# A two-layer decoder on one core: the first layer's maxima subtracted in four row groups, a shorter expert table, and a new order of steps

## The chip, the core and the metric

The kernel runs on one core of a Trainium2 chip. The core has five engines with an instruction queue each: TensorE (PE in the profile; its weight loads are PEld), VectorE (DVE), ScalarE (ACT), GpSimd (POOL) and SyncE (SP), which here only starts transfers. The metric is the device time of one execution in microseconds. Lower is better. The kernel before took 615.67 us, the median of three runs (613.36 to 617.16).

## The reference

The input x has 8 sequences of 256 positions by 256 features. The output is x after six steps, each of the form `x = layernorm(x + step(x))`. Cut to what matters, with all heads 16 wide:

```python
# layer 0
x = ln(x + x @ (Wr + Wc) + bias)                    # mixing with decay matrices
s = (q @ k.T) / sqrt(16)                            # q from x, k and v from 64 context rows; 16 heads
x = ln(x + softmax(where(causal, s, min)) @ v @ Wout)
e = argmax(x @ router_w)                            # one of 8 experts per token
x = ln(x + expert[e](x * sigmoid(max logit)) + shared_expert(x))
# layer 1
x = ln(x + ifft(normed(fft(q)) * cumsum(normed(fft(k)))) @ W_o)
x = ln(x + attention over the 64 context rows (rotary, low rank) )
x = ln(x + rms_norm(silu(x @ Wg) * (x @ Wu)) @ Wp)  # weights rounded to three values
```

A softmax is computed as exp(score - maximum) over its sum. The maximum of each query and head has to be taken off all the head's scores. This is where the change works.

## The kernel before, in words

A sequence is a unit. Units 0 to 7 are the eight sequences in layer 0, and units 8 to 15 are the same eight in layer 1. Five units of layer 0 are in work at a time, and four of layer 1. Between the two layers, all tokens go through the experts: each token's row is sent to a slot of its expert (`rk_send`, an indirect DMA from POOL), a small table says which 128 slots form each of 23 tiles and which expert owns them (`tb_cnt`, `tb_tile`), the tiles are loaded (`x_ld`), multiplied, stored, and gathered back per token (`gt`, indirect DMAs from POOL).

The program is cut into some 2300 steps with short names and (unit, part) numbers. Each step belongs to one engine. `lay_plan` (L334) lists them with a length in units of 10 ns, the steps that they wait for, and the PSUM banks that they need (there are eight). `RANKS` (L173) is a string of two characters for each step that says how urgent it is. `Plan.lay` (L270) walks through time with these lengths and ranks and so fixes, before anything runs, the order of the steps on each engine and the bank of each. On the chip each engine works through its list and waits at each step for the semaphores of that step. A step that is late holds up everything behind it on its engine.

`keep_warm` (L240) then looks for gaps of 0.8 us or more between two PE steps of that plan, and puts filler matmuls into 0.7 of each gap: 128x512 products whose result nobody reads (`warm`, L1418). Its last argument is the time of the plan from which it does so, 9 us.

The steps that matter here, for a unit u:

- Layer 0: `kv`, `turn`, `proj` 0 with `ln` 0, `q`, `max` (scores for the maxima, on PE), `max_v` (the maxima, on DVE, L1913), `mt` (the maxima turned so that heads are rows, L1263), `mt_c` (copied to SBUF by ACT), `sc` (all scores again, minus the maxima, L1268), `ex_h`, `ex_f` and `ex_l` (the exponential and its split), `pv`, `ot`, `proj` 1, then the router `rt`, `rt_top`, `rt_hot` (a one-hot row per token, DVE), `rk` (PE: how many tokens before this one went to the same expert), `rk_seen` (DVE: the running count per expert, L1979), `rk_slot` (DVE: the token's slot), `rk_send` (POOL), and the shared expert `sh`, `sh_h`, `hs_lo`, `proj` 2, `res`, `st_mid`.
- In `sc` of layer 0 four banks are written. A score needs a contraction over 32 rows only, and the four banks' products use different 32 rows of the array (L1277). Then each bank gets the causal mask (L1280, one matmul) and two matmuls that take the maxima off (L1282). These two contract over all 128 rows: `minus_head` has -1 in one of 16 rows and zeros elsewhere.
- `tb` (L1366) sums the counts over the partitions on PE, and `tb_cnt` and `tb_tile` (L2007, L2018) make the table from it with small VectorE instructions. `dve.step` makes the engine wait for its own instruction before the next one.
- Between the layers POOL runs `gt` for four units, `rope` (eight small instructions per unit), and `ln_pow` (the power in the layernorm), which releases `ln_x` on ACT and with it `turn` and `ft` on PE.

## Time and profile before

| | |
|---|---|
| median of 3 runs | 615.67 us (613.36 to 617.16) |
| the profiled execution's own time | 610.82 us |
| its span in the profile | 609.5 us |
| granted TensorE clock, mean | 0.99 |
| PE, DVE, ACT, POOL busy | 553.6, 472.8, 369.8, 389.4 us |
| instructions | 14270 |

The span is the time from the first to the last instruction of the profiled execution. The busy share of PE counts a matmul from its start to its modelled end, so matmuls that follow each other overlap, and a busy PE isn't an engine that has no room. The fillers count as busy too. The start of one matmul less the start of the one before says more.

### The profile page before, as it was taken

How to read it: one execution, taken by the hardware profiler on the slowest of the kernel's cores; microseconds unless marked ns; L12 is line 12 of the kernel's file. 1: busy time of each engine (PE TensorE's matmuls, PEld its weight loads, DVE VectorE, ACT ScalarE, POOL GpSimd, SP SyncE). 2: the span in 40 equal slices, each digit the busy share in tenths (PEclk: the TensorE clock that was granted, in tenths of full speed). 3: DMA queues.
4: the chain of work that ended last, by engine and by line, in shares of the span. 5: the costliest groups of instructions: out<-in, count | busy, mean ns of one | idle time of the engine just before them, and what ended most of it. 6: DMA issues, size and time to landing. Idle time of an engine off the chain costs nothing. (4 is left out here: it accounts for less than half of the span.)

```text
span 609.5 us, 14270 instructions
## 1 busy us (share of the span) xinstructions
PE 553.6 (91%) x5331; PEld 436.6 (72%) x5331; DVE 472.8 (78%) x1266; ACT 369.8 (61%) x783; POOL 389.4 (64%) x467
## 2 busy tenths in 40 slices
PE   5789999889777999977899999999999999999995
PEld 3657887768654766643477888887877778889994
DVE  6896978796889675568899586689888898867656
ACT  5767588667643644545376567647665666655663
POOL 5839657678770440079999938775686644343896
PEclk9998999999899999999899999999999999999999
DMA  9132223104657443472010000022001200000001
GB/s 351 46 140 91 69 74 121 40 24 140 194 173 225 128 146 104 160 170 37 0 31 3 2 1 2 2 54 53 2 20 34 52 3 1 2 1 3 1 2 69
DMA packets 23696, 42.19 MB, mean 69 GB/s; under 512 B 3834, under 2 KB 18300, under 8 KB 23612
## 3 DMA queue, kind: packets, MB, share of 16 engines
q1 hardware_dynamic: 19900, 35.56, 17.9%
q0 software_dynamic: 3072, 4.20, 3.4%
q10 hardware_dynamic: 656, 1.52, 0.8%
q8 instruction: 43, 0.70, 0.5%
q14 instruction: 25, 0.20, 0.1%
HBM read 31.96 MB, written 10.35 MB: 69 GB/s over the span
## 5 line engine op out<-in xcount | busy, mean ns | idle before, releaser
L1761 DVE TENSOR_TENSOR first<-bank,first 128x512 f16<-128x512 f32 (+2 forms) x127 | 69.7, 564 | 14.0 <-ACT first L1627 5.9
L2216 POOL TENSOR_TENSOR first<-first 128x512 f16<-128x512 f32 x44 | 52.5, 1197 | 22.4 <-ACT first L1648 19.7
L1070 PE MATMUL bank<-wide,first 128*128 128x256 f16 (+4 forms) x199 | 54.3, 283 | 8.7 <-DVE first L1761 3.2
L1077 PE MATMUL bank<-c_first,first 128*128 128x128 f32 (+1 forms) x318 | 51.4, 280 | 3.8 <-ACT first L1580 1.8
L1071 PE MATMUL bank<-wide,first 128*128 128x256 f16 (+4 forms) x199 | 54.1, 282 | 0.0
L1072 PE MATMUL bank<-wide,first 128*128 128x256 f16 (+4 forms) x199 | 53.1, 281 | 0.0
L1077 PEld LDWEIGHTS bank<-c_first,first 128*128 128x128 f32 (+1 forms) x318 | 36.3, 140 | 12.2 <-ACT first L1580 4.7
L2194 POOL TENSOR_TENSOR first<-first,minus_half 128x2 f32<-128x2 f32 x30 | 22.3, 744 | 26.9 <-DVE first L1860 26.8
L2239 POOL DMA_INDIRECT wide<-made_rows,made_at x8 | 13.0, 1621 | 38.9 <-DMA made_rows<-first 35.0
L1761 DVE TENSOR_TENSOR wide<-bank,wide 128x512 f16<-128x512 f32 (+1 forms) x52 | 33.1, 651 | 4.8 <-ACT wide L1593 2.4
L2314 POOL TENSOR_TENSOR wide<-wide 128x512 f16<-128x512 f32 x16 | 18.6, 1160 | 23.4 <-ACT wide L1737 23.4
L1070 PEld LDWEIGHTS bank<-wide,first 128*128 128x128 f16 (+1 forms) x199 | 19.4, 100 | 19.5 <-issue 7.0
L1422 PE MATMUL bank<-c_first 128*128 128x512 f16 x126 | 32.9, 388 | 0.0
L1640 ACT ACTIVATE first<-bank 128x512 f16<-128x512 f32 x44 | 25.7, 596 | 11.6 <-PE bank L1282 4.3
L1648 ACT ACTIVATE first<-bank 128x512 f32<-128x512 f32 x44 | 26.3, 598 | 8.5 <-POOL first L2216 8.4
L1455 PE MATMUL bank<-wide,w_fgu 128*128 128x256 f16 x256 | 30.4, 273 | 0.0
L1077 PE MATMUL bank<-c_first,wide 128*128 128x128 f32 (+1 forms) x146 | 23.1, 276 | 8.0 <-POOL wide L2275 4.6
L2250 POOL TENSOR_TENSOR wide<-wide 128x768 bf16<-128x768 bf16 x8 | 13.6, 1698 | 26.2 <-DVE wide L1843 26.2
L1455 PE MATMUL bank<-first,w_fgu 128*128 128x256 f16 x256 | 29.9, 273 | 0.0
L1922 DVE TENSOR_REDUCE first<-bank 128x8 f32<-128x512 f32 x44 | 27.9, 679 | 0.9 <-PE bank L1260 0.9
L1455 PEld LDWEIGHTS bank<-first,w_fgu 128*128 128x128 bf16 x256 | 25.0, 98 | 3.3
L1580 ACT ACTIVATE wide<-wide 128x256 f32<-128x256 f32 x32 | 17.5, 594 | 15.5 <-POOL wide L2196 15.4
(465 smaller groups left out, 2108.4 us busy)
## 6 DMA issues: line engine op xcount, KB each, us to landing
wide<-in_fold SPq DMA_DIRECT2D x8, 992.0 KB, 5.2
wide<-in_expert SPq DMA_DIRECT2D x8, 768.0 KB, 4.7
wide<-in_ternary SPq DMA_DIRECT2D x8, 384.0 KB, 4.1
first<-sent_rows SPq DMA_DIRECT2D x20, 128.0 KB, 2.2
made_rows<-first SPq DMA_DIRECT2D x20, 128.0 KB, 1.9
x_mid<-first SPq DMA_DIRECT2D x7, 256.0 KB, 2.7
first<-in_x SPq DMA_DIRECT2D x4, 256.0 KB, 3.0
wide<-x_mid SPq DMA_DIRECT2D x4, 256.0 KB, 3.0
```

Of the source, the lines that this page charges most:

```text
L1070: mm(o, lhs[0], rhs[0], start=start, stop=False)
L1071: mm(o, lhs[0], rhs[1], start=False, stop=False)
L1072: return mm(o, lhs[1], rhs[0], start=False, stop=stop)
L1077: last = nc.tensor.transpose(view[0:m, c0:c0 + n], src, kc["identity" if dt == F32 else "identity_bf"][0:n, 0:n])
L1422: mm(b[:, 0:4 * P].rearrange("p (n q) -> p n q", n=4), kc["all_ones"], kc["all_ones"].unsqueeze(1).broadcast_to([P, 4, P]), start=True, st ...
L1455: last = mm(b[:, n * S:(n + 1) * S], k.w_fgu[:, c, at:at + P], B.xT[part][:, c, :], start=(c == 0 and part == 0), stop=(c == C - 1 and par ...
L1640: fn(lane(u).ph[g % 2], scores(u, g)[:, :], ACT.Exp, scale=0.25 if u < NB else 1.0).then_inc(says("ex_h"), 1)
L1648: fn(lane(u).pf, scores(u, g)[:, :], ACT.Exp, scale=0.25 if u < NB else 1.0).then_inc(says("ex_f"), 1)
L1761: return V.tensor_tensor(lo, whole, hi, ALU.subtract)
L1922: V.tensor_reduce(o, b, AX.X, ALU.max).then_inc(says("max_v"), 1)
L2194: pool.step(G.tensor_tensor(B.rstd, B.rstd, k.minus_half, ALU.pow))
L2216: G.tensor_tensor(B.pl[r], B.pf, B.ph[r], ALU.subtract).then_inc(says("ex_l"), 1)
```

## The change

It does five things.

1. `sc` of layer 0 takes the maxima off with matmuls over 32 rows, in the four row groups. For that the maxima of heads 4g to 4g+3 have to lie in rows 32g to 32g+3 after `mt`. So `max_v` writes them 32 columns apart into a bf16 tile of 128 columns per 128 tokens, `mt` turns 128x128 bf16 blocks in place of 128x16 f32 ones (in both layers), and `mt_c` copies 128 rows in place of 16. The mask comes last.
2. `rk_seen` isn't run for the last unit: `tb` sums the running count and the last unit's one-hot rows itself, with three matmuls. Its tile `cnt` is f32 in place of f16.
3. `tb_cnt` keeps six instructions, with three waits of the engine for itself in place of five. `tb_tile` has 12 instructions in place of 17, and five such waits in place of nine.
4. Lengths of steps in `lay_plan` are changed, `RANKS` is new, and so is the order of the steps on every engine.
5. Fillers start at 25 us of the plan, not at 9 us.

```diff
-    c["minus_head"] = bf(np.concatenate([np.broadcast_to(sel, (NH, NP, 2, L)).reshape(NH, NP, P), np.zeros((P - NH, NP, P))]))
+    sel = -(row == P // ROWS * (pair // 2) + pair % 2 * 2 + own).astype(np.float32)
+    c["minus_head"] = bf(np.broadcast_to(sel, (P, NP, 2, L)).reshape(P, NP, P))
...
-    ":?:N=87{<:=)=Q=4;h=3;7=&:a<x<8;M8A<l=A<-6g=J=a=7=6='<a=b<i=O=S")
+    ":-<t5(:s<$<z=P<]<|=H:F7q=*;[:.=W;M=)<?;U=-:S<4=@9b<C<V;x=2<~:A")
...
-        p.add("kv", u, 0, "PE", 61, [("ctx_lo", u, 0), ("pt_lo", 0, 2), ("in_id", 0, 0)], k, 1, ("kv_vlo", u, 0))
+        p.add("kv", u, 0, "PE", 100 if u < FIRST else 64, [("ctx_lo", u, 0), ("pt_lo", 0, 2), ("in_id", 0, 0)], k, 1, ("kv_vlo", u, 0))
...
-        p.add("sc", u, 0, "PE", 204, [("mt_c", u, 0), ("kv_vlo", u, 0)], k, 4, [("ex_f", u, g) for g in range(4)])
+        p.add("sc", u, 0, "PE", 140, [("mt_c", u, 0), ("kv_vlo", u, 0)], k, 4, [("ex_f", u, g) for g in range(4)])
...
-        p.add("rk_seen", u, 0, "DVE", 98, [("rt_hot", u, 0)] + before, k - 0.5)
+        if u < NB - 1:
+            p.add("rk_seen", u, 0, "DVE", 34, [("rt_hot", u, 0)] + before, k - 0.5)
...
-    p.add("tb", 0, 0, "PE", 18, [("rk_seen", NB - 1, 0)], 6, 1, ("tb_cnt", 0, 0))
-    p.add("tb_cnt", 0, 0, "DVE", 179, [("tb", 0, 0)] + over, 6)
-    p.add("tb_tile", 0, 0, "DVE", 220, [("tb_cnt", 0, 0), ("in_tab", 0, 0)], 6)
+    p.add("tb", 0, 0, "PE", 20, [("rt_hot", NB - 1, 0), ("rk_seen", NB - 2, 0)], 6, 1, ("tb_cnt", 0, 0))
+    p.add("tb_cnt", 0, 0, "DVE", 110, [("tb", 0, 0)] + over, 6)
+    p.add("tb_tile", 0, 0, "DVE", 190, [("tb_cnt", 0, 0), ("in_tab", 0, 0)], 6)
...
-    p.keep_warm(80, 0.7, 900)
+    p.keep_warm(80, 0.7, 2500)
...
-        B.cnt = a.tile([NE], F16)
+        B.cnt = a.tile([NE])
...
-        flip(bank("mt", u), [(t * P, NH, lane(u).mx[:, t, :]) for t in range(T)]).then_inc(says("mt"), 1)
+        flip(bank("mt", u)[:, :].bitcast(BF16), [(t * P, P, lane(u).mx[:, t, :]) for t in range(T)], BF16).then_inc(says("mt"), 1)
...
-            for n, b in enumerate(banks):
-                mm(b[:, :].rearrange("p (n s) -> p n s", n=2)[:, :, 0:L], kc["identity_bf"], kc["causal_cols"], start=False, stop=False)
-                for m in range(C):
-                    last = mm(b[:, m * S:(m + 1) * S], kc["minus_head"][:, 2 * n + m, :], B.mT, start=False, stop=(m == C - 1))
+            for m in range(C):
+                for n, b in enumerate(banks):
+                    rows = slice(n * PAIR, (n + 1) * PAIR)
+                    mm(b[:, m * S:(m + 1) * S], kc["minus_head"][rows, 2 * n + m, :], B.mT[rows, :], start=False, stop=False)
+            for b in banks:
+                last = mm(b[:, :].rearrange("p (n s) -> p n s", n=2)[:, :, 0:L], kc["identity_bf"], kc["causal_cols"], start=False, stop=True)
...
     def tb(u, g):
-        pe.wait_ge(*done("rk_seen", NB - 1))
-        mm(bank("tb", 0)[:, 0:NE], kc["all_ones"], k.seen[NB], start=True, stop=True).then_inc(says("tb"), 1)
+        pe.wait_ge(*done("rt_hot", NB - 1))
+        pe.wait_ge(*done("rk_seen", NB - 2))
+        counted = [k.seen[NB - 1]] + [lane(NB - 1).hot[:, t, :] for t in range(T)]
+        b = bank("tb", 0)
+        for n, some in enumerate(counted):
+            last = mm(b[:, 0:NE], kc["all_ones"], some, start=(n == 0), stop=(n == T))
+        last.then_inc(says("tb"), 1)
...
-        dve.step(V.tensor_tensor(tab.cnt, bank("tb", 0)[:, 0:NE], kc["region_base"][:, 0, :], ALU.subtract))
-        dve.step(V.memset(tab.ones8, 1.0))
-        dve.step(V.tensor_scalar(tab.cnt_i, tab.cnt, float(P - 1), None, ALU.add))
+        V.memset(tab.ones8, 1.0)
+        dve.step(V.scalar_tensor_tensor(tab.cnt_i, given, float(P - 1), base, ALU.add, ALU.subtract))
+        V.tensor_tensor(tab.cnt, given, base, ALU.subtract)
```

How instructions move, at three places. In these lists a row is an instruction in its engine's order, with the line, the operation, the tiles and, in brackets, the semaphores that it waits for.

PE, the scores of one unit in layer 0. Before (the first two rows are the score products, L1282 takes the maxima off, L1280 adds the mask, L1077 is `mt` of another unit):

```order
L1277 MATMUL bank<-first 128x256 [waits s_max_v]
L1277 MATMUL bank<-first 128x256 x23
L1280 MATMUL bank<-c_rest 128x2x64
L1282 MATMUL bank<-first,c_rest 128x256 x2
L1280 MATMUL bank<-c_rest 128x2x64
L1282 MATMUL bank<-first,c_rest 128x256 x2
L1280 MATMUL bank<-c_rest 128x2x64
L1282 MATMUL bank<-first,c_rest 128x256 x2
L1280 MATMUL bank<-c_rest 128x2x64
L1282 MATMUL bank<-first,c_rest 128x256 x2
L1077 MATMUL bank<-c_first,first 16x128 [waits s_q_lo]
L1077 MATMUL bank<-c_first,first 16x128
```

The same place in the changed kernel:

```order
L1281 MATMUL bank<-first 128x256 [waits s_max_v,s_q_lo,s_mt_c]
L1281 MATMUL bank<-first 128x256 x23
L1286 MATMUL bank<-first,c_rest 128x256 x8
L1288 MATMUL bank<-c_rest 128x2x64 x4
L1081 MATMUL bank<-c_rest,first 128x128 [waits s_max_v]
L1081 MATMUL bank<-c_rest,first 128x128
```

The eight matmuls for the maxima now follow each other bank by bank, each in its own row group, and the masks follow them.

DVE, from the last unit's one-hot rows to the table. Before (L1977 ends `rt_hot` 7, L1986 and L1987 are `rk_seen` 7, L1992 to L1995 are `rk_slot` 7, L1761 is `ed_lo` 7, L2011 begins `tb_cnt`):

```order
L1977 TENSOR_TENSOR first<-c_rest,bank 128x16 [waits own_dve]
L1986 TENSOR_TENSOR first<-first 128x8 [waits s_route_dve]
L1987 TENSOR_TENSOR seen<-first,seen 128x8 [waits own_dve]
L1992 TENSOR_TENSOR first<-bank,first 128x16 [waits s_rk]
L1994 TENSOR_REDUCE bank<-first 128x2 [waits own_dve]
L1995 CAST slot_of<-bank 128x2 [waits own_dve]
L1761 TENSOR_TENSOR wide<-wide 128x512 [waits s_eg_lo,s_ed_hi]
L2011 TENSOR_TENSOR fifth<-bank,c_rest 128x8 [waits s_tb]
```

In the changed kernel (L1993 is the end of `rt_hot` 7, L1772 is `ed_lo` 6, L2008 to L2011 are `rk_slot` 7, L2028 begins `tb_cnt`):

```order
L1993 TENSOR_TENSOR first<-c_rest,bank 128x16 [waits own_dve]
L1772 TENSOR_TENSOR wide<-wide 128x512 [waits s_eg_lo,s_ed_hi]
L2008 TENSOR_TENSOR first<-bank,first 128x16 [waits s_rk]
L2010 TENSOR_REDUCE bank<-first 128x2 [waits own_dve]
L2011 CAST slot_of<-bank 128x2 [waits own_dve]
L2028 MEMSET fifth 128x8 [waits s_tb]
```

`rk_seen` 7 is gone from between the one-hot rows and the slots, and an `ed_lo` (the lower half of an expert's weights, 128x512) has moved there.

POOL, between the layers. Before, from the end of `rope` 8 (L2273, L2275) on; L2194 and L2196 are an `ln_pow`, L2239 is half a `gt`, L2250 an `f_q`:

```order
L2273 TENSOR_TENSOR wide<-wide 128x64 [waits own_pool]
L2275 TENSOR_SCALAR wide<-wide,c_first 128x64 [waits own_pool]
L2275 TENSOR_SCALAR wide<-wide,c_first 128x64
L2194 TENSOR_TENSOR wide<-wide,minus_half 128x2 [waits s_ln]
L2196 TENSOR_TENSOR wide<-wide 128x2 [waits s_ln,own_pool]
L2239 DMA first<-made_rows,made_at 128x256 [waits d_x2]
L2239 DMA first<-made_rows,made_at 128x256
L2194 TENSOR_TENSOR wide<-wide,minus_half 128x2 [waits s_ln]
L2196 TENSOR_TENSOR wide<-wide 128x2 [waits s_ln,own_pool]
L2250 TENSOR_TENSOR wide<-wide 128x768 [waits s_ternary_dve]
L2239 DMA first<-made_rows,made_at 128x256 [waits d_x3]
L2239 DMA first<-made_rows,made_at 128x256
```

In the changed kernel, from `gt` 9 on (L2250 is half a `gt`, L2205 and L2207 are an `ln_pow`):

```order
L2250 DMA wide<-made_rows,made_at 128x256 [waits d_x1]
L2250 DMA wide<-made_rows,made_at 128x256
L2250 DMA first<-made_rows,made_at 128x256 [waits d_x2]
L2250 DMA first<-made_rows,made_at 128x256
L2205 TENSOR_TENSOR wide<-wide,minus_half 128x2 [waits s_ln]
L2207 TENSOR_TENSOR wide<-wide 128x2 [waits s_ln,own_pool]
L2250 DMA first<-made_rows,made_at 128x256 [waits d_x3]
L2250 DMA first<-made_rows,made_at 128x256
L2205 TENSOR_TENSOR wide<-wide,minus_half 128x2 [waits s_ln]
L2207 TENSOR_TENSOR wide<-wide 128x2 [waits s_ln,own_pool]
L2205 TENSOR_TENSOR first<-first,minus_half 128x2 [waits s_ln]
L2207 TENSOR_TENSOR first<-first 128x2 [waits s_ln,own_pool]
```

The third `gt` now stands ahead of the first `ln_pow`, `rope` 8 stands behind all four, and no `f_q` is between them.

Elsewhere: at the start PE ran `kv` of all five units and three fillers before the first `proj`, and now runs `kv` of units 0, 2 and 1. The fillers are 126 matmuls before and 90 now: from the end of the experts' work to the first `q` of layer 1 they are 68 before and 55 now, and from there to the end 23 and 14. Ahead of the experts, 35 are now 21.

## Rows read from the trace of the kernel before

**Rows 1.** The page, engines: busy us, share of the span, instructions.

```profile
PE 553.6 (91%) x5331; PEld 436.6 (72%) x5331; DVE 472.8 (78%) x1266; ACT 369.8 (61%) x783; POOL 389.4 (64%) x467
```

**Rows 2.** Stages: stretch, length, busy us (count) of PE, PEld, DVE, ACT, POOL, clock, DMA.

```profile
17.00:55.00 38.00, 31.57 (x377) 23.64 (x375) 36.08 (x78) 24.96 (x53) 24.46 (x32) 0.96 0.24 84
55.00:173.50 118.50, 106.69 (x1470) 89.56 (x1467) 94.52 (x276) 85.67 (x192) 87.96 (x87) 0.99 0.31 100
173.50:189.50 16.00, 11.60 (x78) 8.83 (x78) 14.88 (x53) 5.43 (x12) 7.77 (x6) 1.00 0.67 224
189.50:261.00 71.50, 67.58 (x454) 45.28 (x455) 45.55 (x109) 36.73 (x106) 12.90 (x9) 1.00 0.47 146
261.00:305.00 44.00, 34.02 (x175) 17.24 (x174) 36.06 (x101) 20.04 (x40) 41.46 (x51) 0.96 0.29 62
305.00:609.00 304.00, 292.11 (x2723) 245.27 (x2721) 235.78 (x627) 186.97 (x361) 205.24 (x254) 1.00 0.07 17
```

**Rows 3.** The same for the fillers, L1422, alone: PE and PEld busy, clock, DMA.

```profile
261.00:305.00 44.00, 15.61 (x63) 6.34 (x63) 0.96 0.29 62
305.00:609.00 304.00, 6.75 (x26) 2.43 (x26) 1.00 0.07 17
```

**Rows 4.** Timeline of PE, `sc` and `mt` in layer 0: start, us, instruction.

```profile
40.00 0.83 PE L1277 MATMUL bank<-first 32*128 32x256 f16 x24
40.76 0.23 PE L1280 MATMUL bank<-c_rest 128*128 128x128 bf16 x1
40.83 0.38 PE L1282 MATMUL bank<-first,c_rest 128*128 128x256 bf16 x2
41.05 0.22 PE L1280 MATMUL bank<-c_rest 128*128 128x128 bf16 x1
41.10 0.38 PE L1282 MATMUL bank<-first,c_rest 128*128 128x256 bf16 x2
41.87 0.38 PE L1077 MATMUL bank<-c_first,first 128*16 128x128 f32 x2
```

**Rows 5.** Timeline of PE at the first `proj`.

```profile
15.35 0.42 PE L1071 MATMUL bank<-wide,first 128*128 128x256 f16 x1
15.57 0.42 PE L1072 MATMUL bank<-wide,first 128*128 128x256 f16 x1
...
17.69 0.27 PE L1070 MATMUL bank<-wide,first 128*128 128x256 f16 x1
17.80 0.27 PE L1071 MATMUL bank<-wide,first 128*128 128x256 f16 x1
```

**Rows 6.** Timeline of DVE at the last unit's counts.

```profile
173.52 3.30 DVE L1986 TENSOR_TENSOR first<-first 128x8 f16<-128x8 f16 x1
176.85 0.16 DVE L1987 TENSOR_TENSOR seen<-first,seen 128x8 f16<-128x8 f16 x1
176.93 0.17 DVE L1992 TENSOR_TENSOR first<-bank,first 128x16 f32<-128x16 f32 x1
```

**Rows 7.** Timeline of POOL in the same stretch.

```profile
175.14 1.64 POOL L2257 TENSOR_TENSOR wide<-wide 128x768 bf16<-128x768 bf16 x1
177.78 1.20 POOL L2223 DMA_INDIRECT sent_rows<-first,slot_of  x1 [0.99 <-DVE slot_of L1995]
```

**Rows 8.** Groups by line and form: count, busy us, mean ns, idle before.

```profile
L1986 DVE TENSOR_TENSOR first<-first 128x8 f16<-128x8 f16 x7 | 6.3, 894 | 0.1
```

**Rows 9.** Waits of SP's queue, 170 to 195 us: us, times, longest.

```profile
SPq L164 <- DMA sent_rows<-first,slot_of: 1.4, 1, 1.4
SPq L1027 <- DVE tile_exp L2039: 0.5, 1, 0.5
```

**Rows 10.** Timeline of POOL between the layers.

```profile
270.85 0.72 POOL L2194 TENSOR_TENSOR wide<-wide,minus_half 128x2 f32<-128x2 f32 x1
...
272.28 2.18 POOL L2239 DMA_INDIRECT first<-made_rows,made_at  x1 [0.17 <-issue]
...
275.76 1.86 POOL L2194 TENSOR_TENSOR wide<-wide,minus_half 128x2 f32<-128x2 f32 x1
```

More of the change, by code:

```diff
@@ L392, in lay_plan @@
             p.add("ed_hi", 0, i, "ACT", 52, landed + unread, rank)
-            p.add("ed_lo", 0, i, "DVE", 64, [("ed_hi", 0, i), ("eg_lo", 0, i)] + over, rank)
+            p.add("ed_lo", 0, i, "DVE", 85, [("ed_hi", 0, i), ("eg_lo", 0, i)] + over, rank)
         elif kind == "w":
@@ L565, in lay_plan @@
             p.add("max_v", u, g, "DVE", 60, [("max", u, g)], k)
-        p.add("mt", u, 0, "PE", 22, [("max_v", u, g) for g in range(4)], k, 1, ("mt_c", u, 0))
+        p.add("mt", u, 0, "PE", 14, [("max_v", u, g) for g in range(4)], k, 1, ("mt_c", u, 0))
         p.add("mt_c", u, 0, "ACT", 26, [("mt", u, 0)], k)
@@ L692, in program @@
     k.one = sb("one", [P, 1])[:]
-    k.seen = [sb(f"seen{u}", [P, NE], F16)[:] for u in range(NB + 1)]
+    k.seen = [sb(f"seen{u}", [P, NE], F16)[:] for u in range(NB)]
     k.tile_rows = sb("tile_rows", [P, 1], I32)[:]
@@ L812, in program @@
     tab.begin, tab.last_at, tab.late_by = (a.tile([NE]) for n in range(3))
-    tab.ex, tab.first, tab.mine, tab.cap, tab.base = (a.tile([1]) for n in range(5))
+    tab.ex, tab.first, tab.mine, tab.cap, tab.begin1, tab.at, tab.at2 = (a.tile([1]) for n in range(7))
+    tab.pick8 = a.tile([NE])
     tab.r_base, tab.r_last, tab.r_late = (a.tile([NW]) for n in range(3))
@@ L1630, in mt_c @@
         act.wait_ge(*done("mt", u))
-        fn(lane(u).mT[0:NH, :], bank("mt", u)[0:NH, 0:S], ACT.Copy).then_inc(says("mt_c"), 1)
+        fn(lane(u).mT, bank("mt", u)[:, :].bitcast(BF16)[:, 0:S], ACT.Copy).then_inc(says("mt_c"), 1)
     def scores(u, g):
@@ L1911, in q_lo, with maxima @@
             rest(B.qT[1][:, g, :], b[:, :], B.qT[0][:, g, :]).then_inc(says("q_lo"), 1)
+    def maxima(u, g):
+        m = lane(u).mx.rearrange("p t (q h) -> p t q h", q=ROWS)
+        return m[:, :, g, 0:4] if u < NB else m[:, g // 2, g % 2 * 2:g % 2 * 2 + 2, 0:4]
     def max_v(u, g):
```

131 lines of the change are left out of this document (64 added, 67 removed).

## The prediction

> **What bounds the kernel now.** I read the page's busy line first, then the stages, then the waits at three places. The page has PE at 91% and nothing else above 78% [rows 1], but PE's share means something else in each stage [rows 2]. From 305 us to the end PE is busy 292.1 of 304 us, DVE 236, POOL 205: layer 1 is bound by PE, and a microsecond of matmuls taken away there is one saved. From 261 to 305 us PE is busy 34 of 44 us, of which 15.6 are fillers [rows 3]. POOL is busy 41.5: this stretch waits for the first gathers and layernorms to come through POOL. From 17 to 55 us DVE is the engine with no room (36.1 of 38 us). From 55 to 173.5 us PE (106.7 of 118.5), DVE (94.5) and POOL (88) are all much used and each unit's chain passes through all of them: less work on one of them is worth only a part. From 173.5 to 189.5 us a single chain decides: DVE 14.9 of 16 us, PE 11.6, ACT 5.4.
>
> **The change, part by part.**
>
> *Maxima in row groups.* At full speed two matmuls with 256 columns and the mask take 0.27 us (one pair starts at 40.83, the next at 41.10), of which the mask with 128 columns is 0.05 [rows 4]: 0.11 us a matmul, 8 a unit, 0.88 us. The 24 score products in row groups start at 40.00 and the next instruction at 40.76: six sets of four in 0.76 us, 0.127 a set [rows 4]. Two more sets are 0.25 us. Per unit 0.88 - 0.25 = 0.63 us, eight units: **5.0 us of PE in layer 0**, and as much off each unit's chain. None of it lies in the stage that PE binds. *Turning the maxima:* two f32 matmuls of 0.11 us (0.38 for both, 0.27 for one) become two bf16 ones of 0.05, like the mask's [rows 4]: 0.11 us for a unit, 0.9 us in each layer. In layer 1 I count it in full, **-0.9**. In layer 0 both together are 5.9 us of PE. Hidden by DVE they are worth 0, all on the chains 5.9 at most. PE has the greatest share of three in 55 to 173.5 us, so I take a third: **-2.0** (0 to -5.9).
>
> *The last unit's counts.* `rk_seen` 7 holds DVE from 173.52 to 177.01 us [rows 6]. Its first instruction takes 3.30 us, and the seven of its form average 0.894 us [rows 8]. It ends at 176.82, as POOL's 128x768 product that began at 175.14 ends (176.78) [rows 7]. Behind it on DVE stands `rk_slot` 7, which releases POOL's last `rk_send` at 177.78 [rows 7]. That transfer's landing is what SP's first `x_ld` waited for last, 1.4 us, and the table only 0.5 us before that [rows 9]. So this stall lies on the path: without it `rk_slot` begins at 173.5 and not at 176.93: **-3.4**. In its place stands `ed_lo` 6, 0.68 us if nothing holds it. It waits for POOL's `eg_lo` 6, which a POOL queue that is late makes later. I take -3.4 + 0.9 = **-2.5** (-3.4 to +0.5).
>
> *Is it the type of the counts?* The seven f16 additions lose 6.3 - 7 x 0.16 = 5.2 us over the undisturbed 0.16 us [rows 6, 8], 3.1 of them in the one that goes. If f32 ended these stalls, DVE would get back another 2.1 us, at a third 0.7. What rows 6 and 7 show is that the stall ends with POOL's product, within 0.04 us, and nothing ties it to the type: I take 0 (0 to -0.7). The Trainium skill (SBUF — State Buffer, Who interferes with whom) says that a DVE instruction with two SBUF inputs contends with a GpSimd instruction that reads SBUF, and that the loser blocks for the whole instruction. Rows 6 and 7 agree with it; by that rule the additions that stay, still with two inputs in SBUF, go on stalling, and the sum gets nothing.
>
> *The table.* Six waits of DVE for itself go and five instructions: at 0.16 to 0.2 us a waited step some 1.2 us. It ends before the last sent rows land, by 0.9 us [rows 9], and both ends move with the step above: **-0.3** (0 to -1.2). If it were late, `x_ld` would be.
>
> *The order at the start.* Until 16 us a matmul with 256 columns takes 0.22 us of PE, and after it 0.11 [rows 5]: PE is at its lower level, 1.2 GHz, though the granted clock reads full. A `kv` there is three of 0.22 and six quarters of that, 0.97 us. Two `kv` and three fillers (0.44 each) leave the front of the first `proj`: 3.2 us of PE. The rest of the way to `proj` (the mixing matrix through DVE, ACT, DVE) isn't shorter by as much: **-1.0** (0 to -3.2).
>
> *Between the layers.* The fillers are the plan's gaps times 0.7, so 13 fewer of 0.22 us are 4.1 us less gap in the plan. On POOL the third `gt` (272.28 to 275.76, 3.5 us) moves ahead of the first `ln_pow` at 270.85 [rows 10]. `rope` 8 no longer stands before it, but it filled a wait. So unit 8 starts some 2 us later, while `ln_pow` 9 comes at about the same time and units 10 and 11 come some 4 and 8 us earlier, as no `f_q` and `rope` stand between. PE then has four units to choose from: **-2.0** (+2 to -4.1).
>
> *The order in layer 1.* 9 fewer fillers are 2.8 us less gap in the plan. What is there to win in the trace: 304 - 292.1 = 11.9 us idle and 26 fillers of 0.22, 5.7 us [rows 2, 3]. The plan is only right as far as its lengths are, so half: **-1.4** (+3 to -6).
>
> *The order in the rest of layer 0 and in the experts.* From 17 to 173.5 us PE is idle for 18 us, and from 189.5 to 261 for 4 [rows 2]. Nothing in the order says how much of it goes: **-2.0** (+4 to -6).
>
> Sum: -2.0 - 0.9 - 2.5 - 0.3 - 1.0 - 2.0 - 1.4 - 2.0 = **-12.1 us** on the profiled execution's 610.8: 598.7. That execution was 0.8% below the median of the runs. The same difference from 615.7 gives **603.6 us**.
>
> **Rivals.** A measurement of this kernel tells about 1% (6.2 us) from no change, so faster begins at 609.5 us and slower at 621.8.
>
> *A, the forecast*, 598 to 609.5 us, chance 0.46 with E below.
>
> *B, the plan comes true:* with lengths nearer to the trace the gaps go on the chip as in the plan, 2.1 us more between the layers, 1.4 in layer 1, 3 in layer 0: 12.1 + 6.5 = 18.6, 597 us. For it: 90 fillers for 126. Against it: most of the early decrease is only the later start of fillers. Chance 0.19.
>
> *C, only what is taken away counts:* -0.9, -2.5 and a microsecond in layer 0, the order neither gains nor loses: 611 us, within 1%. For it: PE is so full in layer 1 that any order is alike, and one late step upsets a list made without knowing of stalls as in rows 6. Chance 0.27.
>
> *D, the lower level stays, slower:* the fillers of the first 25 us kept PE going between the five `proj` and the first `turn`. Without them the engine may stay at 1.2 GHz beyond 16 us. From 17 to 55 us PE is busy 31.6 of 38 us [rows 2]. At half the rate the same matmuls would need up to as much again, of which the idle 6.4 us hide a part and DVE's load more. I take half of the 25 us left, 13, on case C: 624 us. It decides once the level lasts past some 30 us. Against it: all other matmuls there are still issued back to back, and DVE binds. Chance 0.08.
>
> *E, the stall moves:* `ed_lo` 6, now ahead of `rk_slot` 7, is held by POOL as `rk_seen` 7 was, for up to 3.3 us [rows 6]. Then the third term is 0.7 us of loss in place of 2.5 of gain: 607 us. For it: the same engine, at the same place, beside the same kind of POOL work. Against it: POOL's queue there is sends, and it had just done the `eg_lo` that `ed_lo` waits for. Chance 0.06, taken from A's 0.46. By the skill's rule above `ed_lo`, an addition of two SBUF inputs, is open to this.
>
> **The numbers.** Forecast 604 us. Cases A and B are faster: 0.65. C is within: 0.27. D: 0.08. The range leaves out D and the far end of B: **594 to 616 us**. Its upper end is C with the unsure terms of the order at a third of their worst.
>
> **What the profile after would show.** `sc` with 0.25 us between the first and the last of its eight L1286; no DVE instruction above 1 us between the last L1993 and L2011, with the first `x_ld` 2 to 4 us sooner after the last `rt` than now; some of the seven L2002 still far above 0.16 us if the type is no cure; matmuls with 256 columns 0.11 us apart from about 17 us on; the third gather of POOL ahead of the first power, and PE idle less between the layers; in layer 1 PE idle below 12 us over some 300. The prediction is wrong if layer 1 takes longer than 304 us, if the low level lasts, or if the units of layer 0 finish later than at 173 us, since then the new order loses more than all the other terms bring.

## The result, and the profile after

The changed kernel takes **606.24 us**, the median of four runs (604.40 to 608.12), against 616.27 for the kernel before beside it: a ratio of 0.985, with a 95% interval of 0.982 to 0.989. A second comparison, on another chip, gave 605.24 against 611.89, 0.989 (0.985 to 0.993). The gain is 6 to 10 us. The forecast was 604, from a sum of -12.1.

The profiled execution took 608.06 us (span 606.7) against 610.82 (609.5), 2.8 us less. It is one of the changed kernel's longest, and that of before was shorter than all four in the comparison. So I also use a second profile of the changed kernel, from the second comparison, with a span of 603.3 us. The table shows where the time was won and given back, with the start in us unless the row says otherwise. An `x_ld` is counted from the reading of its row of the table, 1.0 us ahead of the first transfer itself.

| | before | changed | changed, second profile |
|---|---|---|---|
| first bias product of `proj` | 16.10 | 15.15 (-1.0) | 13.97 (-2.1) |
| end of the last `rt_hot` | 173.48 | 169.37 (-4.1) | 169.49 (-4.0) |
| first `x_ld` | 183.75 | 176.07 (**-7.7**) | 176.81 (-6.9) |
| first `x_gu` | 192.46 | 188.63 (-3.8) | 189.69 (-2.8) |
| end of the last `x_ld` | 242.94 | 241.05 (-1.9) | 240.78 (-2.2) |
| first `ft` | 276.25 | 280.06 (**+3.8**) | 276.14 (-0.1) |
| the 2600th matmul from the end, fillers left out | 317.42 | 317.77 (+0.4) | 314.67 (-2.7) |
| last matmul | 602.59 | 599.89 (-2.7) | 596.49 (-6.1) |

Up to the first load of the experts the sum is reached: -7.7 and -6.9 us, where the terms for this part are -5.8 and a share of the -2.0 for the rest of the order. Then two waits give most of it back: one ahead of the first `x_gu`, one ahead of layer 1. Behind the first `ft` another 3.4 and 2.6 us are won.

The busy line answers [rows 1]:

```profile
PE 549.2 (91%) x5297; PEld 432.6 (71%) x5297; DVE 465.9 (77%) x1259; ACT 370.4 (61%) x783; POOL 389.6 (64%) x467
```

The stages answer [rows 2], cut near the same events as there: stretch, length, busy us (count) of PE, PEld, DVE, ACT, POOL, then granted clock and DMA.

```profile
17.00:55.00 38.00, 30.97 (x385) 24.48 (x383) 32.47 (x80) 27.42 (x57) 28.10 (x33) 0.89 0.30 100
55.00:169.50 114.50, 101.01 (x1458) 84.44 (x1447) 93.84 (x276) 82.63 (x187) 85.55 (x86) 0.98 0.30 102
169.50:189.00 19.50, 13.46 (x100) 10.09 (x99) 17.97 (x56) 7.76 (x17) 12.32 (x10) 0.94 0.63 208
189.00:261.00 72.00, 69.47 (x440) 45.34 (x438) 41.16 (x100) 34.58 (x99) 7.48 (x5) 0.97 0.40 126
261.00:303.00 42.00, 34.71 (x168) 19.11 (x169) 31.35 (x91) 21.27 (x43) 35.96 (x46) 0.88 0.36 85
303.00:606.70 303.70, 291.64 (x2717) 243.73 (x2715) 239.25 (x636) 186.33 (x358) 210.54 (x259) 0.99 0.07 17
```

The third row isn't to be held against the 16 us of [rows 2]: it ends with the first `x_gu`, and the one there ended 3 us ahead of it. From the last `rt_hot` to the first `x_gu` there are 19.0 us before and 19.3 now, and PE is idle for 6.0 of them now and 5.1 before. The granted clock is lower in every stage than in [rows 2].

PE's timeline at a `sc` of layer 0 answers [rows 4]. From the first of the eight L1286 to the mask there is 0.33 us, and the whole `sc` is issued in 1.2 us; before it took 0.76 and then four times 0.27:

```profile
35.35 0.83 PE L1281 MATMUL bank<-first 32*128 32x256 f16 x24 [0.50 <-DVE first L1938]
36.01 0.40 PE L1286 MATMUL bank<-first,c_rest 32*128 32x256 bf16 x8
36.34 0.40 PE L1288 MATMUL bank<-c_rest 128*128 128x128 bf16 x4
```

PE at the first `proj` answers [rows 5]. Matmuls with 256 columns take 0.42 us, the lower level of 1.2 GHz, up to 19.3 us, 2.8 us longer than before, behind 3.3 us in which PE stood. In the second profile of the same kernel PE stood for 2.4 us, and full rate is there at 16.3 us, so this end moves from run to run:

```profile
14.23 0.37 PE L1074 MATMUL bank<-wide,first 128*128 128x256 f16 x1 [3.34 <-DVE first L1772]
14.40 0.42 PE L1075 MATMUL bank<-wide,first 128*128 128x256 f16 x1
...
19.09 0.42 PE L1075 MATMUL bank<-wide,fifth 128*128 128x256 f16 x1
19.31 0.32 PE L1076 MATMUL bank<-wide,fifth 128*128 128x256 f16 x1
```

VectorE at the last unit's counts answers [rows 6]. `ed_lo` 6 takes 0.73 us, nothing is held, and `rk_slot` 7 begins 0.6 us after `rt_hot`:

```profile
169.20 0.17 DVE L1993 TENSOR_TENSOR first<-c_rest,bank 128x16 f16<-128x16 f32 x1
169.29 0.73 DVE L1772 TENSOR_TENSOR wide<-wide 128x512 f16<-128x512 f32 x1
169.95 0.16 DVE L2008 TENSOR_TENSOR first<-bank,first 128x16 f32<-128x16 f32 x1
```

SyncE's waits in the stretch of [rows 9]. The rows sent are now what the first `x_ld` waits for, and the table, done at 173.11 us, is no longer in the list:

```profile
SPq L931 <- DVE wide L1772: 7.7, 2, 6.1
SPq L165 <- DMA sent_rows<-first,slot_of: 5.5, 1, 5.5
```

Before, it was the other way round than the prediction read it: that list is in order of size and not of time. SyncE was free at 181.66 us, behind a load issued at 181.33, waited 1.4 us for the rows, to 183.0, and then 0.5 us for the table, whose last instruction ends at 183.72, just ahead of the first `x_ld` at 183.75:

```profile
183.58 0.14 DVE L2039 CAST tile_exp<-fifth 128x1 int32<-128x1 f32 x1
```

**The first wait.** VectorE's timeline 8 us later:

```profile
176.85 0.69 DVE L1904 SCALAR_TENSOR_TENSOR first<-bank,first 128x512 f32<-128x512 f32 x1 [0.60 <-PE bank L1076]
177.46 5.86 DVE L1772 TENSOR_TENSOR wide<-wide 128x512 f16<-128x512 f32 x1
```

This is `ed_lo` 7, the same kind of work as the 0.73 us above (4.88 us in the second profile). GpSimd in this time, in a row without a gap that began with one more product at 174.12; `ed_lo` 7 lies beside the last four:

```profile
175.23 2.12 POOL L2198 TENSOR_TENSOR wide<-wide 128x1024 f16<-128x1024 f32 x1
177.31 1.63 POOL L2266 TENSOR_TENSOR wide<-wide 128x768 bf16<-128x768 bf16 x1
178.91 1.15 POOL L2319 TENSOR_TENSOR first<-first 128x512 f16<-128x512 f32 x1
180.03 1.63 POOL L2268 TENSOR_TENSOR wide<-wide 128x768 bf16<-128x768 bf16 x1
181.62 1.14 POOL L2319 TENSOR_TENSOR first<-first 128x512 f16<-128x512 f32 x1
```

`ed_lo` 7 ends at 183.32, 0.56 us behind the last of them (182.76), which is about its own length. Behind it stands `tb_tok` (4.06 us), and behind that the `x_t_lo` for which PE waits, the row of L1074 at 188.63. ScalarE's part of the first rows was ready at 181.2 us (183.9 in the second profile), so it is the two together that hold them up, and `tb_tok` has the greater share:

```profile
184.14 0.38 PE L1081 MATMUL bank<-c_first,fifth 128*128 128x128 f32 x2
188.63 0.61 PE L1074 MATMUL bank<-wide,first 128*128 x1 [4.11 <-DVE first L1772]
```

**The second wait.** PE between the layers. L1121, L1129 and L1137/L1139 are `hm`, `hy` and `hc`, which fold the last weights, and L1433 are fillers:

```profile
264.14 1.47 PE L1433 MATMUL bank<-c_first 128*128 128x512 f16 x6
268.84 1.17 PE L1121 MATMUL bank<-wide 128*96 128x128 f32 x4 [3.23 <-DMA wide<-in_fold]
269.80 1.06 PE L1433 MATMUL bank<-c_first 128*128 128x512 f16 x2
...
275.90 1.89 PE L1433 MATMUL bank<-c_first 128*128 128x512 f16 x4
```

The load of these weights (992 KB) is issued at 261.89 us, before the change at 244.71. The new order does `hc` 4 at 238.9 in place of 208.9 us, and every later fold waits for the one before. PE then stands for 3.2 us, and the matmuls behind run at half their rate (two fillers in 1.06 us, at full rate 0.60), up to 278 us. In the second profile the gap is 0.4 us, and two of the same fillers take 0.60 us again at 270.1. That is where the two profiles of one kernel part, 3.9 us at the first `ft`: 1.3 of them are there when the fold begins (268.84 for 267.56), the rest comes behind it.

### The profile page after: what moved, and what is told of

It reads as the page before. It is cut to its first block and busy times, and to the rows that moved or that the text cites. A ratio compares the mean times of both kernels' runs of the same rounds, so it can differ in the third digit from the quotient of the medians.

```text
span 606.7 us, 14193 instructions
## 1 busy us (share of the span) xinstructions
PE 549.2 (91%) x5297; PEld 432.6 (71%) x5297; DVE 465.9 (77%) x1259; ACT 370.4 (61%) x783; POOL 389.6 (64%) x467
## 5 line engine op out<-in xcount | busy, mean ns | idle before, releaser
L1772 DVE TENSOR_TENSOR first<-bank,first 128x512 f16<-128x512 f32 (+2 forms) x127 | 69.4, 564 | 10.8 <-ACT first L1665 4.4
L1074 PE MATMUL bank<-wide,first 128*128 (+4 forms) x199 | 55.5, 289 | 15.7 <-DVE first L1772 8.9
L1075 PE MATMUL bank<-wide,first 128*128 (+4 forms) x199 | 55.4, 288 | 0.0
L1076 PE MATMUL bank<-wide,first 128*128 (+4 forms) x199 | 54.8, 288 | 0.0
L1081 PE MATMUL bank<-c_first,first 128*128 128x128 f32 x296 | 47.3, 282 | 4.0 <-ACT first L1591 2.7
L2250 POOL DMA_INDIRECT wide<-made_rows,made_at x8 | 12.7, 1584 | 54.5 <-DMA made_rows<-first 47.9
L1081 PEld LDWEIGHTS bank<-c_first,first 128*128 128x128 f32 x296 | 34.9, 144 | 10.9 <-ACT first L1591 3.5
L1074 PEld LDWEIGHTS bank<-wide,first 128*128 128x128 f16 (+1 forms) x199 | 19.8, 101 | 27.2 <-issue 11.3
L1772 DVE TENSOR_TENSOR wide<-bank,wide 128x512 f16<-128x512 f32 (+1 forms) x52 | 33.4, 651 | 7.2 <-ACT wide L1604 3.6
L2205 POOL TENSOR_TENSOR first<-first,minus_half 128x2 f32<-128x2 f32 x30 | 23.2, 772 | 20.1 <-DVE first L1871 19.9
L1651 ACT ACTIVATE first<-bank 128x512 f16<-128x512 f32 x44 | 25.6, 598 | 10.2 <-PE bank L1288 4.5
L1938 DVE TENSOR_REDUCE first<-bank 128x8 bf16<-128x512 f32 x44 | 27.9, 681 | 2.0 <-PE bank L1264 1.4
L1591 ACT ACTIVATE first<-first 128x256 f32<-128x256 f32 x32 | 17.4, 594 | 19.2 <-POOL first L2207 19.2
L2015 DVE SCALAR_TENSOR_TENSOR first<-first,bank 128x256 f32<-128x256 f32 x34 | 14.2, 418 | 17.0 <-ACT first L1699 15.5
L1466 PEld LDWEIGHTS bank<-wide,w_fgu 128*128 128x128 bf16 x256 | 24.8, 98 | 2.8
```

The costliest lines, as they stand in the source:

```text
L1074: mm(o, lhs[0], rhs[0], start=start, stop=False)
L1075: mm(o, lhs[0], rhs[1], start=False, stop=False)
L1076: return mm(o, lhs[1], rhs[0], start=False, stop=stop)
L1081: last = nc.tensor.transpose(view[0:m, c0:c0 + n], src, kc["identity" if dt == F32 else "identity_bf"][0:n, 0:n])
L1466: last = mm(b[:, n * S:(n + 1) * S], k.w_fgu[:, c, at:at + P], B.xT[part][:, c, :], start=(c == 0 and part == 0), stop=(c == C - 1 and par ...
L1651: fn(lane(u).ph[g % 2], scores(u, g)[:, :], ACT.Exp, scale=0.25 if u < NB else 1.0).then_inc(says("ex_h"), 1)
```

## The experiments

The kernel before took 611.2 to 611.9 us in the first three sets and 614.4 in the last, so I compare ratios to it. A ratio between two of our kernels is the quotient of theirs, and its error comes from both intervals.

**1. The changed kernel again.**

> The changed kernel unaltered, beside the others on their chip, since the kernel before took 611.8 us on the chip of the first four experiments and 616.3 on that of the first comparison. If the gain is a property of the order and the instructions, it is again 1.0 to 1.8% below the kernel before. If part of it was that chip's clock, it is less, and the other kernels must be judged against this run alone.

605.24 us, 0.989 (0.985 to 0.993). The gain is real, and here 6.6 us.

**2. All parts under the old order.**

```diff
-    RANKS, lengths in lay_plan, p.keep_warm(80, 0.7, 2500)
+    RANKS, lengths in lay_plan, p.keep_warm(80, 0.7, 900)      # those of before
+        self.order["DVE"].remove(("rk_seen", 7, 0))
```

> All changed instructions (row groups, turned maxima in bf16, short table, no `rk_seen` for the last unit, counts in f32) under the ranks, the lengths and the fillers of the kernel before, so in its order of steps. Theory 1 (as predicted): these are worth 5 to 6 us by themselves, 610 to 611 us, and the order brings the other 4 to 5. Rival 1: the order brings nothing, the parts all: 605 to 607. Rival 2: the parts are lost in the old order's waits and the order brings nearly everything: 614 to 617. Whatever the total: `rk_slot` 7 should begin within 0.3 us of the last `rt_hot` (3.4 us before), and the first `x_ld` 3 to 4 us sooner after the last `rt_hot` than before (10.3 us).

610.40 us, 0.9985 (0.9964 to 1.0006): 0.9 us won, at most 2.2. The prediction had 5 to 6. The expected times were made for a kernel before of 616 us, so the 610.4 only seem to be the first theory; by the ratio it is Rival 2. So the order brings most: 0.9891/0.9985 = 0.991, 5.8 us with an error of 2.8. In its profile (one of its longer runs, a span of 612.8 us) the last `rt_hot` ends at 178.34 us and the first `x_ld` is at 186.65: 8.3 us for 10.3 before, where 3 to 4 us less were expected. The table is again what it waits for last (0.5 us), and `rk_slot` 7 begins 0.45 us behind `rt_hot`, as it waits for PE.

**3. The row groups alone under the old order.**

```diff
     the kernel before
-    mm(..., kc["minus_head"][:, 2 * n + m, :], B.mT, ...)
+    mm(..., kc["minus_head"][rows, 2 * n + m, :], B.mT[rows, :], ...)      # and maxima(), mt, mt_c with it
```

> The kernel before with one part of the change: the maxima written 32 columns apart, turned in bf16 in both layers, and taken off in four row groups. Order, table, counts and fillers are those of before. Under the changed order, undoing the row groups cost 5.2 us (610.46 against 605.24), while all parts together under the order of before gained 1.4 (610.4 against 611.8). Theory 1, what the row groups bring hangs on the order: made with the old lengths, it has PE reach steps whose inputs are late; PE saves 5.0 us in layer 0 and stands as much longer, and the total is within 1.5 us of before. As a sign, the first `sc` take 1.4 us each in place of 2 and more, and PE stands more from 55 to 173 us. Rival (as predicted): a third of the 5.0 us and 0.9 of layer 1 count, 2 to 4 us faster. Second rival, idle time brings the half rate and costs more than is saved: 1 to 3 us slower.

613.80 us, 0.9996 (0.9975 to 1.0017). Nothing is won. The stretch from 70 to 173 us of the kernel before, and of this one behind it (columns as above):

```profile
70.00:173.00 103.00, 91.78 (x1234) 77.22 (x1232) 83.31 (x247) 74.44 (x169) 72.71 (x74) 0.98 0.30 93
```

```profile
70.00:173.00 103.00, 89.86 (x1201) 73.43 (x1200) 82.21 (x241) 74.42 (x167) 71.19 (x72) 0.93 0.28 91
```

PE has less to do, issues less, and the granted clock falls from 0.98 to 0.93. Each `sc` is 0.60 us shorter (1.16 us from its first to its last start, for 1.76). But six of them, 3.6 us, have put PE only 1.2 us ahead at 116 us, and the last `rt_hot` ends 2.1 us later (175.58) than before. In between lies one wait of VectorE whose releaser the trace doesn't name, with which the lead is gone:

```profile
119.13 1.89 DVE L1930 TENSOR_REDUCE first<-bank 128x8 bf16<-128x512 f32 x3 [2.56 <-remote]
```

The profile of number 2, in the same order, has no such wait. So this profile, of the shortest of its 12 runs, shows that most of the saving is hidden before 116 us, but not what becomes of it behind. Some matmuls behind PE's gaps run at half rate, 120 to 124 and 136 to 138 us among them (granted clock 0.50).

**4. The old way of taking off, under the new order.**

```diff
-    row groups of 32 in sc
+    mm(..., kc["minus_head"][:, 2 * n + m, :], B.mT, ...)      # over 128 rows, mask first
```

> The changed kernel with its order, but the maxima are taken off in `sc` as before: mask first, then two matmuls of 256 columns over all 128 rows for each bank (the maxima lie in the same rows of the four groups, so only the time differs). PE has 0.63 us more for each unit of layer 0, 5.0 us in all. Theory 1 (as predicted): a third of it counts, 1.5 to 2.5 us slower than the changed kernel, 608 us. Rival 1, VectorE and the chains hide it: within 0.7 us of 606. Rival 2, it lies on every unit's chain and on the path: 4 to 5 us slower, 610 to 611.

610.46 us, 0.9988 (0.9969 to 1.0007), against the changed kernel 1.010 (1.005 to 1.014): about 6 us slower (3 to 9), which is Rival 2. The two runs were on different chips, with 611.8 and 611.9 us for the kernel before; beside number 6, which was on its chip and is like the changed kernel, it is as much slower (610.46 for 604.45). The row groups, worth nothing under the old order even with the turning in bf16, are worth something like their whole 5 us under the new one.

**5. `rk_seen` 7 taken out of the kernel before.**

```diff
+        self.order["DVE"].remove(("rk_seen", 7, 0))
-    tb: mm(..., k.seen[NB], ...)
+    tb: three matmuls, k.seen[NB - 1] and the two one-hot tiles
```

> The kernel before with one thing changed: the last unit's `rk_seen` isn't run, and `tb` sums the counts with three matmuls. Order, table and all else as before. Theory 1 (as predicted): the 3.3 us stall goes, `rk_slot` 7 begins right behind the last `rt_hot`, the first `x_ld` comes 2.5 to 3.4 us sooner, and the total is 2 to 3 us shorter. Rival 1, the stall goes over to the next instruction of VectorE that works from SBUF to SBUF beside GpSimd, `rk_slot` 7, `ed_lo` 7 or `tb_cnt`: the total is the same within 1 us. Rival 2, the earlier start is lost in the experts: first `x_ld` 3 us sooner, last one not.

611.62 us, 0.9978 (0.9952 to 1.0003): 1.3 us, by interval -0.2 to 2.9. VectorE and GpSimd there:

```profile
174.68 0.16 DVE L2005 CAST slot_of<-bank 128x2 int32<-128x2 f32 x1
175.14 2.04 DVE L1771 TENSOR_TENSOR wide<-wide 128x512 f16<-128x512 f32 x1 [0.31 <-POOL wide L2197]
```

```profile
172.90 2.14 POOL L2197 TENSOR_TENSOR wide<-wide 128x1024 f16<-128x1024 f32 x1
174.98 1.64 POOL L2267 TENSOR_TENSOR wide<-wide 128x768 bf16<-128x768 bf16 x1
176.79 1.26 POOL L2233 DMA_INDIRECT sent_rows<-first,slot_of  x1 [0.17 <-issue]
```

`rk_slot` 7 is done at 174.84, 2.7 us before it was, but the last unit's sends begin at 176.79, only 1.0 us sooner, since GpSimd has two products ahead of them. The first `x_ld` is 0.9 us sooner (182.82). It isn't the sends that hold it, though. Here it doesn't wait for them at all, only for the table:

```profile
SPq L1032 <- DVE tile_exp L2049: 1.2, 1, 1.2
182.65 0.14 DVE L2049 CAST tile_exp<-fifth 128x1 int32<-128x1 f32 x1
```

The table's chain begins behind `ed_lo` 7, and to this the stall goes over in part (2.04 us for 0.69), which is Rival 1; `rk_slot` 7 now waits 0.45 us for PE as well. From the end of `rt_hot` 7 the slots are ready 3.0 us sooner than before (1.0 for 4.0), the table 1.3 us (9.0 for 10.2). The last `x_ld` comes when it did before (0.03 us later), as Rival 2 has it.

**6. Fillers from 9 us on.**

```diff
-    p.keep_warm(80, 0.7, 2500)
+    p.keep_warm(80, 0.7, 900)
```

> The changed kernel with fillers from 9 us of the plan, as before, and not from 25 us. In the changed kernel matmuls run at half rate until 19.2 us, in the one before until 16.3. Theory 1: the fillers' absence is worth little either way; they put up to 1 us ahead of the first `proj` and give back the half rate sooner: 605.5 to 607 us. Rival 1, the fillers held up the front: 2 to 3 us slower, 608 to 609. Rival 2, the longer half rate and the dips of the clock up to 57 us cost more: 1 to 3 us faster, 603 to 605, with full rate from about 16 us.

604.45 us, 0.9903 (0.9875 to 0.9931), the same as the changed kernel within 0.5%, so Theory 1. The matmuls reach full rate at 16.6 us and not at 19.3. But the second profile of the changed kernel had it at 16.3 us without these fillers, so the profiles don't tie it to them.

**7. `ed_lo` 7 moved behind `tb_tok`.** In this and the next ones the step is moved in the finished list; nothing else is planned anew.

```diff
+    order["DVE"]: ..., res 5 2, tb_tok, x_t_lo 2, x_t_lo 0, ed_lo 7, res 6 2, ...
```

> The changed kernel with one step moved in VectorE's list: `ed_lo` 7 (the low half of the eighth expert's second weight, 128x512, read and written in SBUF) stands behind `tb_tok` and the first two `x_t_lo` and not ahead of them. Theory 1, the stall has moved: in the changed kernel `ed_lo` 7 begins at 177.46 us and takes 5.86 us, ending 0.6 us after the last of five GpSimd products in a row, and the first expert product waits 4.1 us for the `x_t_lo` behind it. Moved, it meets an idle GpSimd: it takes about 0.7 us, the first `x_gu` starts near 184.5 and not at 188.6, and the kernel takes 2 to 4 us less than the changed one, 602 to 604 us. Rival, the experts are paced by something later (the seven lanes, the second round of loads): `x_gu` is earlier, the last expert rows aren't, and the time stays at 606 within 0.7 us. Third, the stall goes over to `tb_tok`, whose small instructions also read SBUF twice: nothing is won at all, and they are the long ones.

608.55 us, 0.9945 (0.9924 to 0.9966), slower than the changed kernel by 0.5% (0.1 to 1.0; the chips differ here too). The third case came: now the first small instruction of `tb_tok`, 8 columns, stands, and PE still waits 3.8 us ahead of the first `x_gu` (188.92).

```profile
178.38 4.08 DVE L2062 TENSOR_SCALAR fifth<-fifth 128x8 f32<-128x8 f32 x1
```

```profile
176.98 1.63 POOL L2271 TENSOR_TENSOR wide<-wide 128x768 bf16<-128x768 bf16 x1
178.57 1.15 POOL L2324 TENSOR_TENSOR first<-first 128x512 f16<-128x512 f32 x1
179.69 1.63 POOL L2273 TENSOR_TENSOR wide<-wide 128x768 bf16<-128x768 bf16 x1
181.28 1.15 POOL L2324 TENSOR_TENSOR first<-first 128x512 f16<-128x512 f32 x1
```

It ends at 182.46, GpSimd's row at 182.43. So it is not a matter of the step, and not of two inputs: this instruction has one.

**8. `ed_lo` 7 behind the first `x_t_lo`, `tb_tok` behind the first `x_b_lo`.**

```diff
+    order["DVE"]: ..., res 5 2, x_t_lo 2, ed_lo 7, x_t_lo 0, ..., x_b_lo 0, tb_tok, ...
```

> The changed kernel with two steps moved in VectorE's list: `ed_lo` 7 stands behind the first `x_t_lo`, and `tb_tok` behind the first `x_b_lo`. Where `ed_lo` 7 or `tb_tok` began beside GpSimd's row of products, each was held until the last of them ended (183.3 and 182.5 us). Now VectorE first does an `x_t_lo` that reads PSUM, ready near 181.2, and `ed_lo` 7 only from then on. Theory 1 (the stall is what ate the shorter chain ahead of the experts): `ed_lo` 7 ends by 183.5 and the first `x_gu` begins at 184 to 185 us in place of 188.6; half or more of these 4 us reach the end, 2 to 4 us less than the changed kernel on this chip. Rival, the experts are paced by what follows (seven lanes, DMA, ScalarE): `x_gu` earlier, the last expert rows and the total as in the changed kernel within 1 us.

608.34 us, 0.9938 (0.9906 to 0.9969): not faster. The stall is gone, but I had put `tb_tok` in the experts' way:

```profile
183.45 0.68 DVE L1777 TENSOR_TENSOR wide<-wide 128x512 f16<-128x512 f32 x1
```

```profile
186.55 0.39 PE L1079 MATMUL bank<-wide,first 128*128 x1 [0.55 <-issue]
...
198.75 0.39 PE L1079 MATMUL bank<-wide,first 128*128 x1 [4.10 <-DVE first L1777]
```

The first `x_gu` is at 186.5 us, and from 193.57 to 197.62 VectorE does `tb_tok`, so that the wait of 4.1 us comes ten us later.

**9. The same with fillers from 9 us on.**

> The two moves of the previous kernel and fillers from 9 us of the plan on. Theory 1: the moves' gain comes on top of what the fillers do (the first look at them alone gave 604.45 us against 611.76 before): 2 to 4 us below that, 0.984 to 0.987 of the kernel before. Rival: the two overlap, because both only let the experts begin sooner: 0.990, as the fillers alone.

606.01 us, 0.9906 (0.9872 to 0.9939), as the fillers alone, with the same gap (4.15 us, to 198.25).

**10. `tb_tok` where VectorE has nothing to do.**

```diff
+    order["DVE"]: ..., res 5 2, x_t_lo 2, ed_lo 7, x_t_lo 0, ..., x_b_lo 21, tb_tok, ho_lo 5, ...
```

> The changed kernel with two steps moved in VectorE's list: `ed_lo` 7 behind the first `x_t_lo`, as in the experiment before, but `tb_tok` behind the last `x_b_lo`, where VectorE has nothing to do for 5 us. In the experiment before the first `x_gu` began 3 us sooner (186.5 us for 189.6), and then `tb_tok`, in the middle of the experts, held VectorE for 4.05 us, and PE stood for 4.2 us behind it. Theory 1, the time of the experts follows VectorE's list: with `tb_tok` out of the way there is no such gap, the last `x_ld` comes 3 to 4 us before the changed kernel's (240.8), and the total is 2 to 4 us less: 601 to 603.5 us against 605.2. Rival, what comes behind the experts (the fold of the last weights, whose load waits for its slot, and the gathers) sets the start of layer 1: the last `x_ld` comes sooner and the total stays within 1 us.

**602.36 us, 0.984 (0.981 to 0.988)**, the fastest of all. The first `x_gu` is at 187.3, no gap follows, and the last `x_ld` ends at 236.96, 3.8 us before the changed kernel's. With `ed_lo` 7 out of the way VectorE has nothing to do here, until ScalarE has its part of the first rows:

```profile
183.92 0.42 DVE L1777 TENSOR_TENSOR first<-bank,first 128x256 f16<-128x256 f32 x1 [4.37 <-ACT first L1700]
```

So the stall of `ed_lo` 7 by itself costs the experts little. It cost because `tb_tok` stood behind it.

But the first `ft` is only 0.05 us sooner than in the second profile, since now the fold waits longer:

```profile
258.56 1.47 PE L1438 MATMUL bank<-c_first 128*128 128x512 f16 x6
264.82 0.68 PE L1126 MATMUL bank<-wide 128*96 128x128 f32 x4 [4.79 <-DMA wide<-in_fold]
266.07 1.87 PE L1134 MATMUL bank<-wide 96*128 96x64 f32 x8
```

**11. More fillers ahead of the last fold, and 12. both.**

```diff
-    6 fillers ahead of hm 7
+    12 fillers ahead of hm 7
```

> The changed kernel with 12 fillers in place of 6 ahead of the last fold (`hm` 7), 1.3 us more at the full rate. The changed kernel's runs fall into two groups, at 604 and 607.5 us, and so do the two profiles: in the one of 608.06 us PE stands for 3.4 us before `hm` 7, until the load of its weights (`in_fold`) has landed, and the matmuls behind it run at half rate until 278.4 us, so that unit 8 begins at 280.1; in the other the fillers themselves run at half rate, the gap is 0.8 us, full rate is back at 268.5, and unit 8 begins at 276.1. Theory 1, the gap brings the half rate: with it filled nearly all runs are of the lower group, 603.5 to 605.5 us. Rival, the groups come from the load's landing: both groups stay. Third, the fillers themselves hold up the fold: all runs 1 to 2 us later than the lower group.

605.70 us, 0.992 (0.989 to 0.995). The two groups stay, 605.3 to 605.7 and 608.3 to 608.8, each 1.2 to 1.4 us later than on that chip without: the rival, and the third case on top. So filling the gap is no cure, and what makes the two groups, the load's landing or the rate of the fillers ahead of it, stays open. The gap alone doesn't make the upper one: the profile of number 6 has 4.6 us of it and half rate up to 275.5 us, and is a run of the lower group (604.36).

> Both edits of the two previous kernels together. If both theories hold, this beats the changed kernel by 3 to 5 us, 600 to 602.5 us, with few runs above 604. If only one holds, it is like that one.

603.09 us, 0.986 (0.983 to 0.988), like number 10 alone.

By its own interval number 10 isn't told from the changed kernel (0.995, 0.990 to 1.001). But the move is in two kernels and missing in their two partners (1 and 11): a mean of 0.9851 against 0.9905, a difference of 0.54% with an error of 0.34, 3.3 us. With the first comparison of the changed kernel (0.985) as a third partner it is 0.37% with an error of 0.31, 2.3 us. So the move seems to be worth 2 to 3 us, just clear of the noise.

## Why the prediction was right, and where its steps were off

The time lies in the range and on the forecast side, between the forecast and case C. That is nearer than the sum deserves. Of its -12.1 us the second comparison shows 6.6, and in the profiles the terms up to the last `x_ld` are -1.9 and -2.2 for -7.8, those from there into layer 1 (to the 2600th matmul from the end) +2.3 and -0.5 for -2.0, and those behind -3.0 and -3.4 for -2.3. Step by step:

- **Maxima in row groups, -2.0 (0 to -5.9).** The price on PE was right: each `sc` is 0.60 us shorter for the 0.63 said, 4.8 us in all. Its worth isn't a fixed share. Under the old order it is 0 (number 3: +1.0 to -1.5 us), under the new one about 6 us (number 4), the two ends of the bounds. The third that I took fits neither. Why isn't shown in full: the new order has new lengths and new ranks, and no run has one without the other.
- **The last unit's counts, -2.5.** The stall is gone and rival E did not come at `ed_lo` 6, but the price was wrong: 1.3 us for the kernel (-0.2 to 2.9), 0.9 at the first `x_ld`. I priced the stall by its length, 3.4 us, on a path that wasn't the last: I had read [rows 9] as if the sent rows came last, and it was the table, by 0.7 us. Taken alone (number 5), the edit gives the slots 3.0 us, but the table only 1.3, since the stall goes over to `ed_lo` 7 ahead of it. The stretch from `rt_hot` to the first `x_ld` is 10.3 us before, 9.0 in number 5, 8.3 in number 2 with the shorter table, and 6.7 and 7.3 in the changed kernel: 1.3 us from the counts, 0.7 from the rest of the parts and 1.0 to 1.6 from the order, by one profile each.
- **The type of the counts, 0, and the table, -0.3.** One of the seven L2002 still takes 1.11 us and six 0.15 to 0.18; of the seven L2003 behind them one takes 1.06. Neither was tried alone. The table was on the path before, and in the changed kernel it is done some 3 us ahead of the rows. The groups of the profile, count and durations (least, median, most):

```profile
L2002 DVE TENSOR_TENSOR first<-first x6: 156/163/1109, 80.1 to 165.9; 128x8 f32<-128x8 f16 x6
```

- **The start, -1.0.** -1.0 at the first `proj`, and -2.1 in the second profile. The low level lasts 2.8 us longer in the one and ends 0.4 us sooner in the other. Rival D did not come, and number 6 shows no cost of this end beyond its error of 0.5%.
- **The order of the rest, -2.0.** Up to the first `x_ld` the terms above were -5.8 with a part of this one on top, and the traces have -7.7 and -6.9. In the experts 5.8 and 4.7 us of them are lost again, 4.1 and 2.9 as one wait of PE. This is the step that failed. Rival E named the mechanism, a step of VectorE from SBUF to SBUF held beside GpSimd's products, and I looked for it at one instruction only, with a price of 3.3 us. It came at the next one of the same kind, for 5.2 us (4.2 in the second profile), because the new order had gathered six GpSimd products in a row behind the sends, four of them beside `ed_lo` 7. What made it dear was `tb_tok` behind it, 4 us ahead of the first rows' `x_t_lo`; numbers 7, 8 and 10 point to this, as the time came back only where `tb_tok` went to a gap. The stall of 3.3 us before had lain beside two such products, the one at 175.14 in [rows 7] and this one:

```profile
173.06 2.14 POOL L2187 TENSOR_TENSOR wide<-wide 128x1024 f16<-128x1024 f32 x1
```

  I had not asked how many stand together in the new list.
- **Between the layers, -2.0 (+2 to -4.1).** -2.2 at the last `x_ld` became -0.1 at the first `ft` in one profile, and -1.9 became +3.8 in the other. By the 2600th matmul 2.6 and 3.4 us of this are won back, which fits the forecast that the first unit comes late and the next ones sooner. But the sum of both is -0.5 and +2.3, not -2.0. I had read GpSimd's queue there [rows 10], and the queue was indeed shorter (the first `ln_pow` at 270.70, as before). I had not looked at the weights: the last fold's load had moved 17 us back. What was late next was a DMA and not an engine.
- **Layer 1, -0.9 and -1.4.** The last 2600 matmuls without fillers take 285.2 us before, 282.1 and 281.8 after: -3.0 and -3.4 for -2.3 predicted. Under the old order they take 284.8 and 284.9 with the turning in bf16 (numbers 2 and 3), so the turning is worth 0.3 to 0.4 us for the 0.9 counted in full, and the order 2.7 to 3 for the 1.4.

Rival C said that the order brings nothing and the removals all. It was the other way round: 0.9 us from the removals alone, some 6 from the order with them (8 by the first comparison). The order alone, without the parts, was not run.

## What to carry to other kernels

Price a stall by the path that ends last, not by its own length. Find in order of time what the next stage waits for, since a list of waits by size doesn't tell it, and ask which instruction takes over the stall when this one goes. Where instructions become shorter in a list that was ordered by lengths, expect little until the list is made anew, and then look in the new list for what was put close together, here four products of GpSimd beside a VectorE step that works in SBUF, and for loads that were pushed back. A block of small instructions that nobody needs soon (`tb_tok`, 4 us) belongs where its engine has a gap: moving it there was worth 2 to 3 us, just clear of the noise, and the two other places tried only moved the wait.
